# First attention, last four units: the mask under the scores written by TensorE in place of ScalarE

## The chip, the cores and the metric

The kernel runs on one core of one Trainium2 chip. The metric is the device time of the program in microseconds (us), the median of several executions. Five engines run their own instruction streams and meet at semaphores: TensorE (PE) multiplies matrices and writes to PSUM, VectorE (DVE) and ScalarE (ACT) do elementwise work and reductions, GpSimd (POOL) some elementwise work, SyncE (SP) issues DMAs.

## What is computed

One decoder layer on 16 sequences of 128 tokens, model width 256, in three parts, each added to x: a self-attention, a cross-attention to a context, and a mixture of 16 experts with a shared expert. The change touches only the self-attention, called first attention here:

```python
q = (x @ Wq) -> 16 heads of 128;  k, v = (x @ Wk), (x @ Wv) -> 4 heads of 128;  rope on q and k
q1, q2 = halves of q;  k1, k2 = halves of k
s1 = q1 k1^T / 8;  s2 = q2 k2^T / 8
allowed = (j <= i) & (j >= i - 63)
s1, s2 = where(allowed, s, -1e30)
a1, a2 = softmax(s1), softmax(s2)
diff = relu(a1 - lam[head] * a2)
diff = diff / (sum(diff) + 1e-6)
x = x + (diff v) @ Wo
```

The mask lets a token see itself and the 63 before it. It enters as a sum: PSUM holds 0 or -1e30 for each score, and the score products are added to it.

## The kernel before, in words

First attention goes over 4 groups of heads (4 query heads share a key and value head), and in each group over 16 units, one for each sequence. The groups are written as a first one, a loop over the middle ones, and a final one. Four units make a chunk; while one chunk is attended, TensorE projects the keys, queries and values of the next in the gaps between a unit's steps ("slots" 0, 1 and 2 of a unit). The last chunk of the final group has no next one. Its slots hold the start of the next stage: the layer norm's transposes ("ln"), the merging of the cross-attention's weights ("prep", six steps, TensorE lines L690 and L698, taken by ScalarE into wbh and by VectorE into wbl or mq), and transposes of the context ("kt2", L567).

A unit has two score maps, s1 and s2, of 384 columns each: early queries see only 64 keys, so the map of 4 heads is 128 partitions by 384. Each of the two maps has its own bank, and two pairs of banks (A_S) take turns, so unit u writes to those of unit u-2. In the order in which a unit n goes through the engines:

- TensorE, slot 0, then the 16 score products (L647; the profile counts 32, since each is done in two passes), added to the mask that lies in PSUM; then the transposes of the weights of unit n-2 (L661, L663), slot 1, the product with the values for unit n-2 (L670), the output projection of unit n-3 (L679), slot 2.
- VectorE: the difference of the two maps of unit n-1 (L1072), then the negated maxima of unit n (L1126, L1127), then what the slots need.
- ScalarE: the copy pt of the transposed weights (L1401), the clipping with its sum of unit n-1 (L1478), the 8 exponentials of unit n with their sums (L1434), the copy oah of the output (L1401), and last the copy of the mask into the banks just read (L1489, shown as L1401, since all copies go through one helper).
- GpSimd: the normalisation of unit n-2 (L1665), for which TensorE's transposes wait.

The order is written out by hand in each engine's stream; each engine takes its instructions strictly in that order. The mask copy of unit n serves unit n+2: it raises the semaphore a_mk, for which TensorE waits before the scores (the line `wait(pe, a_mk, n - 1)`). The mask copy itself waits for the exponentials of its own unit (a_ex). Only the first two units of all have no earlier unit to write their mask. For these TensorE writes it by a product of the identity with the mask in bf16 (L643), which starts the sum; the score products then add to it. The last two units of the final group write no mask, since none follows.

Of the kernel before, what the change touches and what calls it, by code (L numbers as in the profile page):

```python
# [18 lines left out]
CB = 4  # L19
NC = B // CB  # L20
# [3 lines left out]
UN = B  # L24
# [75 lines left out]
def wait(eng, sem, value):  # L100

    if isinstance(value, int) and value <= 0:
        return
    eng.wait_ge(sem, value)


def decoder_kernel(nc, x, ctx_in, in_wqk, in_wv, in_wo, in_lam, in_taba, in_rawb, in_tabb, in_kvtab,
# [5 lines left out]
    def sem(name):  # L113
        return ctx.enter_context(nc.semaphore(name))
# [4 lines left out]
    with ctx:  # L119
# [106 lines left out]
        def bank(n):  # L226
            return ps[:, n, :]

        def quads(ap):
            return ap.rearrange("p (h k) -> p h k", k=S)  # L230
# [17 lines left out]
        a_sc, a_mx, a_ex = sem("a_scores"), sem("a_negmax"), sem("a_exp")  # L248
        a_mk = sem("a_mask_in_place")
# [50 lines left out]
        def a_part(first, final, drain):  # L300
            return "first" if first else "final" if final else "drain" if drain else ""
# [90 lines left out]
        def early(ap):  # L392
            return ap[..., 0:XP * QH].rearrange("... (p k) -> ... p k", k=QH)

        def late(ap):
            return ap[..., XP * QH:SW].rearrange("... (p k) -> ... p k", k=S)
# [128 lines left out]
        def _(pe):  # L525
# [8 lines left out]
            def ln_turn(m, kt, bk):  # L534

                pe.wait_ge(ln_xt, m + 1)
                for j in range(CB):
                    last = pe.transpose(quads(bank(bk))[:, j, :], xnt[:, m % 2, j, 128 * kt:128 * (kt + 1)], idf[:, :])
                last.then_inc(ln_tp, 1)

            def ln_ready(m):
                pe.wait_ge(ln_l, m + 1)
                pe.wait_ge(ln_l2, m + 1)
# [11 lines left out]
            def pj_taken(what):  # L555
                if what[0] == "ln":
                    pe.wait_ge(ln_h, 2 * what[1] + what[2] + 1)
                elif what[0] == "prep":
                    pe.wait_ge(b_if, what[1] + 1)
                else:  # L560
                    pe.wait_ge(b_kvc, what[1] + 1)

            def b_turn(r):

                pe.wait_ge(b_kv, 5)
                for j in range(CB):
                    last = pe.transpose(quads(bank(PJ))[:, j, :], kvr[:, CB * r + j, :, :], idf[:, :])  # L567
                last.then_inc(b_kvp, 1)
# [26 lines left out]
            def a_unit(g, u, first=False, final=False, drain=False):  # L595
                n, c, j = g * UN + u, u // CB, u % CB

                def slot(s):
                    if not drain and (j, s) in A_SLOT and not (final and c == NC - 1):
                        ahead = c == NC - 1  # L600
                        if held:
                            pj_taken(held.pop())
                        if first and not ahead and A_SLOT[j, s] == 0:
                            ln_ready(c + 1)
                        a_project(g + 1 if ahead else g, (c + 1) % NC, A_SLOT[j, s], ahead)
                    for what in A_EXTRA.get((a_part(first, final, drain), u, s), []):
                        if what[0] == "qb":
                            if what[1] == 0:
                                pe.wait_ge(a_ex, NG * UN)
                                ln_ready(NC)  # L610
                            b_do(0, 0, what, XT + what[1])
                            continue
                        if held:
                            pj_taken(held.pop())
                        else:

                            ahead = [i for k, i in A_SLOT.items() if k <= (j, s)]
                            if final and c == NC - 1:
                                ahead = []
                            pe.wait_ge(a_pf, (g * NC + (c + 1)) * AW + len([i for i in ahead if i != AV]))  # L620
                            pe.wait_ge(a_vf, g * NC + (c + 1) + (AV in ahead))
                        if what[0] == "ln":
                            ln_turn(what[1], what[2], PJ)
                        elif what[0] == "prep":
                            b_prep(0, what[1], bank(PJ)).then_inc(b_it, 1)
                        else:
                            b_turn(what[1])
                        held.append(what)
                slot(0)
                if first and u == 1:  # L630
                    for kt in range(KT):
                        ln_turn(2, kt, OB + kt)
                if not drain:
                    if j == 0:
                        pe.wait_ge(a_pf, (g * NC + (c + 1)) * AW)
                        pe.wait_ge(a_vf, g * NC + (c + 1))
                        pe.wait_ge(a_kd, 64 * (g * NC + (c + 1)))
                    wait(pe, a_mk, n - 1)
                    tok = slice(S * j, S * (j + 1))
                    for m in range(2):  # L640
                        sc = A_S[u % 2][:, m, 0:SW]
                        if first and u < 2:
                            pe.matmul(sc, idb[:, :], maskb[:, :], start=True, stop=False, skip_group_check=True)  # L643
                        for at, to, keys in ((QH, late(sc), S), (0, early(sc), QH)):
                            for h in range(HG):
                                rows = slice(QH * (h % 2), QH * (h % 2) + QH)
                                last = pe.matmul(to[rows, h // 2, :],  # L647
                                                 qab[:, c % 2, m, h, S * j + at:S * j + at + QH],
                                                 kva[:, c % 2, m, S * j:S * j + keys],
                                                 start=False, stop=at == 0, skip_group_check=True)  # L650
                    last.then_inc(a_sc, 1)
                two = not (first and u < 2) and not (drain and u >= 2)
                if two:
                    pe.wait_ge(a_dn, n - 1)
                    wait(pe, a_pt, n - 2)
                    if first and u == 2:
                        pe.wait_ge(ln_h, 2 * 2 + KT)
                    if first and u == 2:
                        pe.wait_ge(a_ptz, 1)
                    for p in range(XP):  # L660
                        pe.transpose(quads(bank(PTB))[0:QH, p, :], early(ea[:, u % 2, 0, :])[:, p, :], idf[:, :])  # L661
                    for p in range(XP):
                        last = pe.transpose(quads(bank(PTB))[:, XP + p, :], late(ea[:, u % 2, 0, :])[:, p, :], idf[:, :])  # L663
                    last.then_inc(a_tp, 1)
                slot(1)
                if two:
                    w = (u - 2) % UN
                    pe.wait_ge(a_pt, n - 1)
                    wait(pe, a_ol, n - 2)
                    pe.matmul(bank(OB), quads(kva[:, (w // CB) % 2, 2, :])[:, w % CB, :],  # L670
                              pt[:, u % 2, :, :], start=True, stop=True).then_inc(a_pv, 1)
                if not (first and u < 3):
                    if u == 3:
                        pe.wait_ge(a_wol, g + 1)
                    pe.wait_ge(a_ol, n - 2)
                    wait(pe, a_y, n - 3)
                    for h in range(HG):
                        for i, (o_, w_) in enumerate(((oah, woh), (oah, wol), (oal, woh))):
                            last = pe.matmul(ps[:, YB, 0:DM], o_[:, (u - 3) % 2, h, :], w_[:, h, :],  # L679
                                             start=h == 0 and i == 0, stop=h == HG - 1 and i == 2)  # L680
                    last.then_inc(a_wo, 1)
                slot(2)
# [716 lines left out]
        def _(act):  # L1399
            def copy(dst, src):  # L1400
                return act.activation(dst, src, ACT.Copy)  # L1401
# [36 lines left out]
            def a_unit(g, u, first=False, final=False, drain=False):  # L1438
                n, c, j = g * UN + u, u // CB, u % CB
# [43 lines left out]
                if two:  # L1483
                    act.wait_ge(a_pv, n - 1)
                    wait(act, a_wo, n - 3)
                    copy(by_head(oah[:, (u - 2) % 2, :, :]), by_block(bank(OB))).then_inc(a_o, 1)
                if not drain and not (final and u >= UN - 2):
                    act.wait_ge(a_ex, n + 1)
                    copy(A_S[u % 2][:, :, 0:SW], maskb[:, :].unsqueeze(1).broadcast_to([128, 2, SW])).then_inc(a_mk, 1)  # L1489
                if first and u == 1:  # L1490
# [439 lines left out]
```

## Time and profile before

| | us |
|---|---|
| median of 3 runs | 1346.26 |
| lowest, highest | 1346.21, 1348.62 |
| span of the profiled execution (first to last instruction) | 1343.3 |
| TensorE, ScalarE, VectorE, GpSimd busy | 1269.2, 715.6, 843.1, 470.9 |
| mask copies of ScalarE, 62 | 52.8 |

Of the profiled execution the profile gives the span and no time of its own that counts what lies outside of it; the median of the runs is 3.0 us above the span. Times in the rows are us from the start of the span. First attention ends at about 502 us, and its final group's last four units are between 443 and 486 us. PE's busy time counts overlapping products by a modelled end, so the distance from one start to the next says more of its pace than the durations. The granted clock of TensorE is 1.00 at 2.4 GHz and 0.50 at 1.2 GHz.

### The profile page before, as it was taken

The page shows a single profiled execution, that of the slowest core. Times are in us where ns is not written, and L with a number is a line of the kernel's source. Part 1 is how long each engine was busy: PE and PEld are TensorE (multiplying, and loading weights), DVE is VectorE, ACT ScalarE, POOL GpSimd, SP SyncE. Part 2 cuts the span into 40 slices and gives each one's busy share as a digit, 9 for nine tenths or more (in the row PEclk, how much of TensorE's full clock was granted, in tenths as well). Part 3 has the DMA queues.
Part 4 walks back from the last instruction along what each step waited for, and adds up shares of the span by engine and source line. Part 5 has one row for each costly group of instructions (what it writes and reads, how often), then busy time and mean ns, then how long its engine had stood idle before and what let it go on. Part 6 is the DMA issues. An engine that isn't in the chain of part 4 may idle for free.

```text
span 1343.3 us, 27486 instructions
## 1 busy us (share of the span) xinstructions
PE 1269.2 (94%) x9712; PEld 989.2 (74%) x9712; DVE 843.1 (63%) x1986; ACT 715.6 (53%) x2746; POOL 470.9 (35%) x467
## 2 busy tenths in 40 slices
PE   5799999999999788999999999989899999999998
PEld 4578888888887565666666666557788888888887
DVE  6788888888888676666656656765453333433333
ACT  2788888889887553444444444465232332423322
POOL 3122113112212134544544534541053353533532
PEclk9999999999999899999999999999999999999999
DMA  6011001100102101002002001000325342254230
GB/s 221 16 25 49 18 17 25 49 17 17 31 19 92 35 1 76 1 1 76 1 1 75 1 1 60 1 1 1 107 58 142 74 120 56 39 137 78 56 93 31
DMA packets 29810, 64.54 MB, mean 48 GB/s; under 512 B 6912, under 2 KB 12160, under 8 KB 28416
## 3 DMA queue, kind: packets, MB, share of 16 engines
q1 hardware_dynamic: 29696, 63.05, 17.6%
q8 instruction: 67, 1.10, 0.3%
q14 instruction: 47, 0.39, 0.1%
HBM read 52.42 MB, written 2.23 MB: 41 GB/s over the span
## 4 chain that ended last, share of the span: by engine, by line
PE 74%; DVE 10%; ACT 7%; issue 4%; POOL 2%; DMA 2%; SPq 1%; DVEq 0%; POOLq 0%; ACTq 0%
PE ps L531 31%; PE ps L923 9%; PE ps L647 5%; PE ps L716 4%; PE ps L679 4%; PE ps L820 4%; ACT ea L1434 3%; PE ps L810 3%; PE ps L792 3%; PE ps L800 2%; PE ps L670 2%; PE ps L586 2%; DMA cw<-comb_d 2%; ACT ea L1478 1%; DVE xnt L991 1%
## 5 line engine op out<-in xcount | busy, mean ns | idle before, releaser
L1798 POOL TENSOR_TENSOR sg<-sg,cw 128x512 f32<-128x512 f32 x88 | 113.5, 1290 | 260.1 <-ACT sg L1597 253.1
L1375 DVE TENSOR_TENSOR hh<-ps,sg 128x512 f32<-128x512 f32 x100 | 69.2, 692 | 178.6 <-POOL sg L1798 162.0
L1401 ACT ACTIVATE hhh<-hh 128x512 fp32r<-128x512 f32 x100 | 63.2, 632 | 214.7 <-DVE hh L1375 214.7
L1401 ACT ACTIVATE pt<-ps 128x512 f32<-128x512 f32 x128 | 76.9, 600 | 179.3 <-PE ps L800 122.6
L1434 ACT ACTIVATE ea<-ps,negmax 128x64 f32<-128x64 f32 (+1 forms) x512 | 164.6, 341 | 6.0 <-DVE negmax L1127 6.0
L531 PE MATMUL ps<-xnh,wch 128*128 128x512 f32 x400 | 157.0, 393 | 0.7 <-ACT pt L1401 0.7
L1174 DVE TENSOR_TENSOR qcs<-ps,tabb 128x512 f32<-128x512 f32 x192 | 123.6, 686 | 53.4 <-PE ps L531 53.1
L531 PE MATMUL ps<-xnl,wch 128*128 128x512 f32 x400 | 156.9, 392 | 0.0
L531 PE MATMUL ps<-xnh,wcl 128*128 128x512 f32 x400 | 155.6, 389 | 0.0
L1665 POOL TENSOR_TENSOR ea<-ea,rden 128x128 f32<-128x128 f32 (+1 forms) x128 | 62.1, 506 | 256.2 <-DVE rden L1083 256.2
L1672 POOL TENSOR_TENSOR eb<-eb,rsum 128x512 f32<-128x512 f32 x64 | 66.9, 1045 | 160.3 <-DVE rsum L1218 160.3
L923 PE MATMUL ps<-wch,hhh 128*128 128x256 f32 x400 | 115.9, 290 | 4.7 <-DVE hhl L1377 2.4
L1377 DVE TENSOR_TENSOR hhl<-hh,hhh 128x512 fp32r<-128x512 f32 x100 | 75.5, 755 | 69.8 <-ACT hhh L1401 69.8
L923 PE MATMUL ps<-wch,hhl 128*128 128x256 f32 x400 | 113.6, 284 | 0.0
L923 PE MATMUL ps<-wcl,hhh 128*128 128x256 f32 x400 | 113.6, 284 | 0.0
L1434 ACT ACTIVATION_READ_ACCUMULATOR ea<-ps,negmax 128x1 f32 x512 | 107.1, 209 | 0.0
L1434 ACT ACTIVATE eb<-ps,negmax 128x128 f32<-128x128 f32 x256 | 90.5, 368 | 29.4 <-DVE negmax L1212 29.1
L1088 DVE TENSOR_TENSOR x_sb<-ps,x_sb 128x256 f32<-128x256 f32 x128 | 54.1, 423 | 82.1 <-PE ps L820 58.4
L647 PEld LDWEIGHTS ps<-kva,qab 128*64 128x64 f32 x2048 | 93.2, 139 | 13.1 <-issue 7.9
L647 PE MATMUL ps<-kva,qab 128*64 128x128 f32 (+1 forms) x2048 | 102.4, 254 | 0.0
L679 PE MATMUL ps<-woh,oah 128*128 128x256 f32 x256 | 97.6, 381 | 0.7 <-DVE oal L1118 0.7
L1597 ACT ACTIVATE sg<-ps 128x512 f32<-128x512 f32 x100 | 59.9, 599 | 71.5 <-PE ps L531 70.6
(153 smaller groups left out, 3349.6 us busy)
## 6 DMA issues: line engine op xcount, KB each, us to landing
raw_w<-in_rawb_dram SPq DMA_DIRECT2D x4, 2432.0 KB, 9.0
kva<-ktmp SPq DMA_DIRECT2D x64, 128.0 KB, 2.4
cw<-comb_d SPq DMA_DIRECT2D x32, 256.0 KB, 5.0
raw_w<-in_rawc_dram SPq DMA_DIRECT2D x4, 1920.0 KB, 8.0
cw<-comb_d SPq DMA_DIRECT2D x16, 224.0 KB, 4.3
raw_a<-in_wqk_dram SPq DMA_DIRECT2D x4, 768.0 KB, 5.4
cw<-comb_d SPq DMA_DIRECT2D x16, 192.0 KB, 6.0
cw<-comb_d SPq DMA_DIRECT2D x16, 160.0 KB, 5.5
```

The lines of the kernel that those rows point to most:

```text
L531: last = pe.matmul(out_ap, w, m, start=n == 0, stop=n == len(steps) - 1)
L647: last = pe.matmul(to[rows, h // 2, :], qab[:, c % 2, m, h, S * j + at:S * j + at + QH], kva[:, c % 2, m, S * j:S * j + keys], start=False ...
L679: last = pe.matmul(ps[:, YB, 0:DM], o_[:, (u - 3) % 2, h, :], w_[:, h, :], start=h == 0 and i == 0, stop=h == HG - 1 and i == 2)
L923: last = pe.matmul(ps[:, j // 2, DM * (j % 2):DM * (j % 2 + 1)], h_[:, par, S * j:S * (j + 1)], w_[:, t, 2 * KT * 128:RC_T], start=begin a ...
L1174: last = dve.tensor_tensor(quads(qcs[:, t, m, :]), quads(bk), bcast(tabb[:, b_table(t), m, :]), ALU.mult)
L1375: dve.tensor_tensor(hh[:, par, :], bank(C_U[par]), sg[:, par, :], ALU.mult).then_inc(c_h, 1)
L1377: dve.tensor_tensor(hhl[:, par, :], hh[:, par, :], hhh[:, par, :].bitcast(f32), ALU.subtract)\
L1401: return act.activation(dst, src, ACT.Copy)
L1434: last = act.activation(dst(m, h), src, ACT.Exp, bias=negmax[:, par, i:i + 1], accum_out=sums[:, par, i:i + 1])
L1665: last = pool.tensor_tensor(part, part, rden[:, par, XP * i:XP * (i + 1)].unsqueeze(2) .broadcast_to([128, XP, (QH, S)[i]]), ALU.mult)
L1672: pool.tensor_tensor(src[:, par, :, :], src[:, par, :, :], rec[:, par, :].unsqueeze(2).broadcast_to([128, HG, S]), ALU.mult).then_inc(done, 1)
L1798: pool.tensor_tensor(sg[:, par, :], sg[:, par, :], cw[:, c % 2, t, :], ALU.mult).then_inc(c_hs, 1)
```

## The change

In the final group, TensorE writes the mask of units 12 to 15 by the product that the first two units use, two products a unit, one for each map. ScalarE's copies behind units 10 to 13 of that group, which wrote it, are left out. For these units TensorE waits for the exponentials of the unit two before (a_ex), since a_mk is not raised for them. `CB` is 4, `UN` 16 and `NC` 4.

```diff
--- before.py
+++ after.py
@@ -635,11 +635,15 @@
                         pe.wait_ge(a_pf, (g * NC + (c + 1)) * AW)
                         pe.wait_ge(a_vf, g * NC + (c + 1))
                         pe.wait_ge(a_kd, 64 * (g * NC + (c + 1)))
-                    wait(pe, a_mk, n - 1)
+                    by_pe = (first and u < 2) or (final and c == NC - 1)
+                    if final and c == NC - 1:
+                        wait(pe, a_ex, n - 1)
+                    else:
+                        wait(pe, a_mk, n - 1)
                     tok = slice(S * j, S * (j + 1))
                     for m in range(2):
                         sc = A_S[u % 2][:, m, 0:SW]
-                        if first and u < 2:
+                        if by_pe:
                             pe.matmul(sc, idb[:, :], maskb[:, :], start=True, stop=False, skip_group_check=True)
                         for at, to, keys in ((QH, late(sc), S), (0, early(sc), QH)):
                             for h in range(HG):
@@ -1484,7 +1488,7 @@
                     act.wait_ge(a_pv, n - 1)
                     wait(act, a_wo, n - 3)
                     copy(by_head(oah[:, (u - 2) % 2, :, :]), by_block(bank(OB))).then_inc(a_o, 1)
-                if not drain and not (final and u >= UN - 2):
+                if not drain and not (final and u >= UN - CB - 2):
                     act.wait_ge(a_ex, n + 1)
                     copy(A_S[u % 2][:, :, 0:SW], maskb[:, :].unsqueeze(1).broadcast_to([128, 2, SW])).then_inc(a_mk, 1)
                 if first and u == 1:
```

ScalarE's stream in the final group, behind the exponentials of unit 10 and then of unit 11. The names read out<-in; kva takes the values of the last chunk, wbh the high part of the merged weights. Before:

```order
L1401 ACTIVATE oah<-ps 128x2x4x64
L1401 ACTIVATE ps<-maskb 128x2x384
L1401 ACTIVATE kva<-ps 128x512
L1401 ACTIVATE xnf<-ps 128x512
L1401 ACTIVATE xnh<-ps 128x512
...
L1401 ACTIVATE oah<-ps 128x2x4x64
L1401 ACTIVATE ps<-maskb 128x2x384
L1401 ACTIVATE wbh<-ps 128x4x64
L1401 ACTIVATE wbh<-ps 128x4x32
L1401 ACTIVATE pt<-ps 128x512
```

After:

```order
L1405 ACTIVATE oah<-ps 128x2x4x64
L1405 ACTIVATE kva<-ps 128x512
L1405 ACTIVATE xnf<-ps 128x512
L1405 ACTIVATE xnh<-ps 128x512
...
L1405 ACTIVATE oah<-ps 128x2x4x64
L1405 ACTIVATE wbh<-ps 128x4x64
L1405 ACTIVATE wbh<-ps 128x4x32
L1405 ACTIVATE pt<-ps 128x512
```

The two mask copies are gone, and kva and wbh follow oah directly; two more go likewise behind units 12 and 13.

TensorE's stream around the scores of unit 12, from the merging product of prep 0 to that of prep 1. Before:

```order
L690 MATMUL ps<-raw_w 128x192 x2
L647 MATMUL ps<-kva,qab 64x128 x4
L647 MATMUL ps<-kva,qab 64x64 x4
L647 MATMUL ps<-kva,qab 64x128 x4
L647 MATMUL ps<-kva,qab 64x64 x4
L661 MATMUL ps<-idf,ea 64x128 x2
L663 MATMUL ps<-idf,ea 128x128 x2
L690 MATMUL ps<-raw_w 128x192 x2
```

After:

```order
L694 MATMUL ps<-raw_w 128x192 x2
L647 MATMUL ps<-maskb,idb 128x384
L651 MATMUL ps<-kva,qab 64x128 x4
L651 MATMUL ps<-kva,qab 64x64 x4
L647 MATMUL ps<-maskb,idb 128x384
L651 MATMUL ps<-kva,qab 64x128 x4
L651 MATMUL ps<-kva,qab 64x64 x4
L665 MATMUL ps<-idf,ea 64x128 x2
L667 MATMUL ps<-idf,ea 128x128 x2
L694 MATMUL ps<-raw_w 128x192 x2
```

A mask product stands ahead of each map's score products; the same holds for units 13, 14 and 15. From L647 on, TensorE's line numbers are higher by four in the changed kernel. The instructions of the other engines keep their order.

## Rows read from the trace of the kernel before

**Rows 1.** The page: the chain that ended last, by engine.

```profile
PE 74%; DVE 10%; ACT 7%; issue 4%; POOL 2%; DMA 2%; SPq 1%; DVEq 0%; POOLq 0%; ACTq 0%
```

**Rows 2.** The mask's instructions: count, ns min/median/max, first and last start us.

```profile
L1401 ACT ACTIVATE ps<-maskb x62: 814/850/882, 35.8 to 462.5; 128x768 f32<-128x768 bf16 x62
```

**Rows 3.** The chain of waits, units 10 to 15: start us, us, what.

```profile
428.09 1.38 PE ps L531 x6
...
433.55 0.80 issue
...
442.75 0.70 ACT ps L1401
...
465.88 1.71 PE ps L698 x20
467.58 2.76 PE ps L647 x32
470.34 0.57 PE ps L661 x2
470.91 0.44 PE ps L663 x2
...
477.28 1.49 PE ps L647 x32
```

**Rows 4.** ScalarE's timeline: start us, us, instruction, idle before and its releaser.

```profile
432.89 0.85 ACT L1401 ACTIVATE ps<-maskb 128x768 f32<-128x768 bf16 x1
433.62 0.63 ACT L1401 ACTIVATE kva<-ps 128x512 f32<-128x512 f32 x1
...
442.57 0.88 ACT L1401 ACTIVATE ps<-maskb 128x768 f32<-128x768 bf16 x1
443.43 0.55 ACT L1401 ACTIVATE wbh<-ps 128x256 fp32r<-128x256 f32 x2
445.48 0.60 ACT L1401 ACTIVATE pt<-ps 128x512 f32<-128x512 f32 x1 [1.49 <-PE ps L663]
446.32 0.26 ACT L1478 ACTIVATE ea<-ea 128x64 f32<-128x64 f32 x1 [0.25 <-DVE ea L1072]
...
452.95 0.55 ACT L1401 ACTIVATE wbh<-ps 128x256 fp32r<-128x256 f32 x2 [1.25 <-PE ps L690]
...
471.38 0.60 ACT L1401 ACTIVATE pt<-ps 128x512 f32<-128x512 f32 x1 [7.98 <-PE ps L663]
471.87 0.25 ACT L1478 ACTIVATE ea<-ea 128x64 f32<-128x64 f32 x1
```

**Rows 5.** TensorE's timeline, the first unit of all, and what follows it.

```profile
29.50 0.32 PE L643 MATMUL ps<-maskb,idb 128*128 128x384 bf16 x1 [1.69 <-DVE qab L1032]
...
30.58 0.34 PE L643 MATMUL ps<-maskb,idb 128*128 128x384 bf16 x1
...
31.66 0.50 PE L531 MATMUL ps<-xnh,wah 128*128 128x512 f32 x1
```

**Rows 6.** TensorE's timeline, units 10 to 13 of the final group.

```profile
431.60 1.95 PE L586 MATMUL ps<-wv,xnf 128*128 128x128 f32 x16
...
442.58 0.81 PE L690 MATMUL ps<-raw_w 128*128 128x192 f32 x4
...
451.28 1.63 PE L690 MATMUL ps<-raw_w 128*128 128x192 f32 x4 [2.61 <-DVE wbl L1181]
452.84 2.46 PE L647 MATMUL ps<-kva,qab 128*64 128x128 f32 x32
456.36 0.41 PE L661 MATMUL ps<-idf,ea 128*64 128x128 f32 x2 [1.07 <-POOL ea L1665]
```

**Rows 7.** Busy time by stretch: us, PE busy, granted clock, DMA share, GB/s.

```profile
453.00:454.00 1.00, 1.00 (x14) 0.50 0.04 8
466.00:468.00 2.00, 2.00 (x25) 0.50 0.00 0
472.00:473.00 1.00, 1.00 (x4) 1.00 0.00 0
```

## The prediction

> **What bounds the kernel now.** I read the chain of waits of the whole program first. TensorE holds 74% of it and ScalarE 7% [rows 1], so work added to TensorE costs time unless a wait covers it, and work taken from ScalarE gives something only where ScalarE is late. Then I listed the instructions that read the mask: 62 mask copies of 850 ns each, the last at 462.5 [rows 2]. The change removes the last four of them, so 3.4 us of ScalarE's time is the most that could come back. Which of the four is on the path is read from the chain over the last units of first attention [rows 3]: it names a mask copy once, for 0.70 us at 442.75, and an "issue" of 0.80 us at 433.55, behind which a second one could hide. So I looked at each copy's neighbours in ScalarE's timeline [rows 4].
>
> **What is removed.** I call the last sixteen units 0 to 15; the removed copies stand behind the exponentials of units 10 to 13, and fed units 12 to 15. The wait of TensorE that each satisfied never ended last: a copy starts two units ahead of its scores (432.89 against scores behind the product of 442.58, 462.5 against 477.28) [rows 2, 3, 4, 6]. What counts is the ScalarE instruction behind each copy.
> - Copy at 432.89: the next one, the copy of the values into kva, starts 0.73 us later, at 433.62 [rows 4], which looks as if it waited for the mask copy. But the projection that it reads starts at 431.60 and takes 1.95 us, so it ends at 433.55 [rows 6]. Without the mask copy it would start 0.07 us earlier at most, and less the 0.04 us that such a release takes (452.91 to 452.95 below), 0.03 us. TensorE's transposes behind the "issue" wait for that copy. Gain 0.03.
> - Copy at 442.57: the next, wbh, starts at 443.43 [rows 4]. The product that it reads starts at 442.58 and takes 0.81 us, so it ends at 443.39 [rows 6]; 0.04 us later wbh starts. The same distance stands where wbh was plainly waiting for TensorE: idle 1.25 us, ended by L690 at 452.95 [rows 4], whose product ran from 451.28 for 1.63 us, to 452.91 [rows 6]. So here TensorE released it, and the 0.70 us that the chain charges to the mask copy is not to be had. Gain 0; bound above, 0.12 us: a mask copy alone holds its follower for 0.73 to 0.74 us, which would be 443.31.
> - Copies behind units 12 and 13: ScalarE is idle behind them, 1.25 us until 452.95 and 7.98 us until 471.38 [rows 4]. Gain 0.
>
> The sum of the gains is 0.03 us, between 0 and 0.15.
>
> **What is added.** Eight products, mask by identity, 128x384 in bf16, two ahead of each of units 12 to 15, with their weight loads. The first units have the same pattern. There a map with its mask product takes from 29.50 to 30.58 = 1.08 us, and the unit of two maps from 29.50 to 31.66 = 2.16 us [rows 5]. A unit without them takes 1.49 us at 477.28 [rows 3]. So a pair costs 2.16 - 1.49 = 0.67 us of TensorE at full clock. At the lower one, the 32 score products take 2.76 us in place of 1.49 [rows 3], a factor of 1.85, so the pair costs 0.67 x 1.85 = 1.24 us; the bound is twice, 1.34.
>
> Against this stands a rule of the Trainium skill. "TensorE: Matmul & The Clock Gate", section "Back-to-back issue gap", gives N / 2.4 + 2.5 ns between starts at full clock and N / 1.2 at the low one. For 384 columns that is an estimate of 0.16 and 0.32 us a product, and half of what the rows show for the pair. The trace's first units measure this very sequence and include what the change of operands does to the score products behind it, so I go by them; the cheaper result is a rival below.
>
> Unit by unit, in TensorE's order, with what covers it:
> - Unit 12 (scores behind the product of 442.58, full clock): +0.67 on the transposes and on ScalarE's copy pt at 445.48. Behind it ScalarE's clipping starts at 446.32, having waited for VectorE's difference. With VectorE out of the way it starts 0.49 us after pt (471.38 to 471.87). So the cover is 0.84 - 0.49 = 0.35 us [rows 4], and 0.67 - 0.35 = 0.32 us passes to the exponentials and through them to wbh and VectorE's chain up to unit 13. VectorE's maximum is behind that same difference, so it hides the later scores.
> - Unit 13 (scores at 452.84, low clock at first): TensorE is idle 1.07 us behind the scores until GpSimd's normalisation ends [rows 6]. The pair costs at most 1.24. The clock is at 0.50 in 453 to 454 [rows 7], and rises in the midst of the scores, whose 32 took 2.46 us and not 2.76 [rows 3, 6], so part of the pair's cost falls at full clock. I take 0, with 0.17 (1.24 - 1.07) as the upper bound.
> - Unit 14 (scores at 467.58, low clock): the chain runs through the product of prep, the scores, both pairs of transposes and ScalarE [rows 3], with nothing idle. The pair costs 1.24. The clock is at 0.50 in 466 to 468 and 1.00 in 472 to 473 [rows 7]; work pushed past the rise runs faster. The transposes would be pushed there: 0.57 + 0.44 = 1.01 us [rows 3], and 1.01 / 1.85 = 0.55 at full clock, which is 0.46 to get back at most. I take half, so 1.24 - 0.23 = 1.01, between 0.67 and 1.34.
> - Unit 15 (scores at 477.28, full clock): on the chain with the transposes and ScalarE behind them [rows 3]. +0.67.
>
> Nothing behind waits for a fixed time, and TensorE leads the chain from there on, so a shift at the end of the stage is carried to the end. No DMA is moved. The new wait, for the exponentials of two units before, was implied by the old one, and queues nothing new.
>
> **Sum.** -0.03 + 0.32 + 0 + 1.01 + 0.67 = +1.97 us. The profiled execution spans 1343.3 us, and the median of the runs is 1346.26, 3.0 us more, which I take to stay. The forecast is 1346.26 + 1.97, about 1348.2 us, 0.15% slower. With the bounds, the sum is 0.67 at the least for unit 14 and 1.34 at the most: -0.15 + 0.32 + 0 + 0.67 + 0.67 = 1.5, up to 0.32 + 0.17 + 1.34 + 0.67 = 2.5, so 1347.8 to 1348.8, and somewhat wider, 1347.3 to 1349.3, for the spread of the runs. What a measurement of this kernel can tell from no change is 0.2%, 2.7 us; the forecast is within it.
>
> **Rivals.**
> - The product is cheap. Six projections of 512 columns take 1.38 us, 0.23 each from 428.09 [rows 3]; 384 columns at that rate are 0.17 us, 0.35 the pair, and 0.35 x 1.85 = 0.64 at the low clock. Then unit 12's is just covered, unit 13's too, and 0.64 + 0.35 = 1.0: 1347.2 us. For it: nothing but the first units shows the dear one. Against it: both maps of the first unit take the same 1.08 us [rows 5], so it was no accident of the first product. The gap formula of the Trainium skill, "TensorE: Matmul & The Clock Gate", would lead to this case.
> - The added work prolongs the low clock (the slower side). Place: unit 14. If the clock has not risen by the time that unit 15 starts, then unit 15's scores take 2.76 in place of 1.49, its pair 1.24 and its transposes 0.46 more. In sum 0.32 + 1.24 + 1.27 + 1.24 + 0.46 = 4.5: 1350.8 us, 0.34% slower. It decides from the point where the granted clock is below 1.00 at the scores of unit 15. Against it: TensorE is busier there than before, and the clock was back at 1.00 in 472 to 473, four us ahead of unit 15's scores [rows 3, 7].
> - The clock stays up ahead of unit 14, since TensorE is busier. The chain's stretch from 465.88 is at the low clock, behind one in which TensorE did little. At full clock the scores save 1.27, the transposes 0.46, prep's products 1.71 - 1.71 / 1.85 = 0.79 [rows 3], and the pair costs 0.67: 0.32 + 0.67 + 0.67 - 2.52 = -0.9: 1345.4 us. Against it: the change adds nothing to TensorE's work between unit 13's scores and 465.88.
> - The copies were on the path as the chain says: 0.73 and 0.70 us come back, and the products are mostly covered by the idle time so won (left 0.3): 1346.26 - 1.43 + 0.3 = 1345.1 us. Against it: the 0.04 us distances above.
>
> **Chances.** Forecast 0.60, cheap product 0.14, longer low clock 0.12, clock stays up 0.08, copies on the path 0.06. Faster by over 0.2% (below 1343.6) none of the cases reaches; 0.04 for what I don't see. Slower by over 0.2% (above 1348.95): the 0.12, and a fifth of the forecast's, 0.12, so 0.24. Within: 0.72. The range 1345.3 to 1349.8 leaves out most of the longer low clock and little at the lower end; the likeliest case's own is 1347.3 to 1349.3.
>
> **What would show it.** In the profile after: eight more products of mask by identity beside the four, 58 mask copies of some 850 ns. Unit 12 to its transposes 2.16 us in place of 1.49, and the clipping behind it waiting for VectorE no longer. wbh still 0.04 us behind the product that it reads: if it starts a good 0.1 us earlier, the copy was late after all. TensorE's wait for GpSimd at unit 13 shrunk from 1.07 but not gone. Units 14 and 15 longer by 1.2 and 0.67. The start of unit 15's last exponentials against unit 10's some 2 us later than before. The forecast is wrong if the granted clock of 465 to 480 has other low stretches than before, or if the pair costs near 0.35.

## The result and the profile after

| | median, us | lowest to highest | runs | ratio to before, 95% |
|---|---|---|---|---|
| before | 1347.05 | 1346.08 to 1348.62 | 7 | |
| changed | 1351.11 | 1348.68 to 1352.11 | 7 | 1.0026, 1.0017 to 1.0036 |

The ratios here and below are not the quotients of the two medians, and differ from them by up to 0.06%, 0.8 us; here the quotient is 1.0030.

The change makes the kernel slower by 0.26%, where 0.15% was forecast, and the median lies 1.3 us above the upper end of the range. The spans rose from 1343.3 to 1350.3 us, but the profiled execution of the changed kernel was its slowest, 1352.11 us. The first lines of the page, and the chain by engine, answer to [rows 1]:

```profile
span 1350.3 us, 27498 instructions
...
PE 72%; DVE 10%; ACT 8%; issue 4%; DMA 3%; POOL 2%; SPq 1%; DVEq 0%; POOLq 0%; ACTq 0%
```

What the changed kernel's trace says of the mask answers to [rows 2] (ns min/median/max, first and last start):

```profile
L1405 ACT ACTIVATE ps<-maskb x58: 814/852/863, 36.4 to 428.4; 128x768 f32<-128x768 bf16 x58
...
L647 PE MATMUL ps<-maskb,idb x12: 323/337/527, 29.5 to 482.4; 128*128 128x384 bf16 x12
```

Four copies are gone and eight products have come. The longest of the products, 527 ns, is not one at full clock: the four of the kernel before took 322 to 337 ns. The chain of waits shows where they stand (start us, us, what); it answers to [rows 3]. The first row is a stretch ahead of everything that was changed:

```profile
423.85 2.56 PE ps L531 x6
...
446.22 0.16 PE ps L647
446.38 0.82 PE ps L651 x16
447.20 0.27 PE ps L647
447.47 0.82 PE ps L651 x16
...
470.65 0.43 PE ps L647
471.08 1.48 PE ps L651 x16
472.56 0.43 PE ps L647
473.00 1.48 PE ps L651 x16
474.48 0.38 PE ps L665 x2
474.86 0.23 PE ps L667 x2
...
481.03 0.16 PE ps L647
481.19 1.29 PE ps L651 x16
482.48 0.43 PE ps L647
482.92 1.48 PE ps L651 x16
484.40 0.54 PE ps L665 x2
```

A unit's pair shows as two L647 rows, its scores as two L651 rows. Unit 12 takes 446.22 to 448.29 on the chain with everything at full clock. Unit 14, from 470.65 to 474.48, takes 3.83 us against 2.76. Unit 15, from 481.03 to 484.40, takes 3.37 us against 1.49 [rows 3]. In unit 12 the second product takes 0.27 us and each half of the scores 0.82; in unit 15 they take 0.43, 1.29 and 1.48. TensorE's clock fell within its first half. The granted clock by stretch (us, PE busy, clock, DMA share, GB/s) answers to [rows 7]:

```profile
424.00:426.00 2.00, 2.00 (x6) 0.50 1.41 320
470.60:474.50 3.90, 3.90 (x39) 0.50 0.00 0
475.20:478.00 2.80, 2.55 (x16) 1.00 0.03 6
480.40:481.30 0.90, 0.90 (x9) 1.00 0.00 0
482.00:485.00 3.00, 3.00 (x32) 0.54 0.00 0
```

The low stretch at unit 14 is there as before. The one of 482 to 485, over unit 15's scores, is new. In the kernel before, unit 15's scores ran in full clock:

```profile
476.60:479.20 2.60, 2.58 (x41) 1.00 0.00 0
```

ScalarE's timeline answers to [rows 4], with the one row of before that was not shown, unit 15's pt:

```profile
436.49 0.60 ACT L1405 ACTIVATE kva<-ps 128x512 f32<-128x512 f32 x1 [0.75 <-PE ps L586]
...
446.26 0.55 ACT L1405 ACTIVATE wbh<-ps 128x256 fp32r<-128x256 f32 x2 [0.67 <-PE ps L694]
448.88 0.60 ACT L1405 ACTIVATE pt<-ps 128x512 f32<-128x512 f32 x1 [2.07 <-PE ps L667]
449.38 0.25 ACT L1482 ACTIVATE ea<-ea 128x64 f32<-128x64 f32 x1
...
475.11 0.60 ACT L1405 ACTIVATE pt<-ps 128x512 f32<-128x512 f32 x1 [9.36 <-PE ps L667]
...
485.19 0.60 ACT L1405 ACTIVATE pt<-ps 128x512 f32<-128x512 f32 x1 [3.04 <-PE ps L667]
```

```profile
479.37 0.60 ACT L1401 ACTIVATE pt<-ps 128x512 f32<-128x512 f32 x1 [0.96 <-PE ps L663]
```

TensorE's timeline answers to [rows 6], and its last row shows the idle gap ahead of unit 15. Below it stands the same row of before, with the same gap:

```profile
434.50 1.95 PE L586 MATMUL ps<-wv,xnf 128*128 128x128 f32 x16
...
445.41 0.81 PE L694 MATMUL ps<-raw_w 128*128 128x192 f32 x4
...
459.42 0.41 PE L665 MATMUL ps<-idf,ea 128*64 128x128 f32 x2 [0.64 <-POOL ea L1669]
...
480.37 0.66 PE L538 MATMUL ps<-idf,xnt 128*128 128x128 f32 x4 [2.05 <-ACT xnh L1405]
```

```profile
476.62 0.66 PE L538 MATMUL ps<-idf,xnt 128*128 128x128 f32 x4 [2.04 <-ACT xnh L1401]
```

With these rows the difference can be followed from place to place (starts in us):

| place | before | changed | shift |
|---|---|---|---|
| projection of the values, unit 10 | 431.60 | 434.50 | 2.90 |
| prep's first product, unit 11 | 442.58 | 445.41 | 2.83 |
| pt, unit 12 | 445.48 | 448.88 | 3.40 |
| clipping, unit 12 | 446.32 | 449.38 | 3.06 |
| transposes, unit 13 | 456.36 | 459.42 | 3.06 |
| pt, unit 14 | 471.38 | 475.11 | 3.73 |
| pt, unit 15 | 479.37 | 485.19 | 5.82 |
| span | 1343.3 | 1350.3 | 7.0 |

So 2.9 us had gone before the first changed instruction, and 1.2 us go behind the last one, all of it between 1000 and 1200 us, where the later traces lose anything from 0 to 0.9 against before (e3 below, which has no added product, 0.8). In the changed units the trace loses 5.82 - 2.90 = 2.92 us: +0.23 at unit 12 after a gain of 0.07, 0 at unit 13, +0.67 at unit 14, and +2.09 at unit 15.

The executions of a kernel differ in where TensorE's clock is low. The runs give the mean granted clock of each: of the kernel before, 0.989 to 0.993, mean 0.990 over 27 runs; of the changed kernel, in 13 runs of two measurements, 0.988 eleven times, 0.989 once, and 0.992 in its fastest run of 1348.68 us. The profiled execution of before was of a rarer kind: its clock is 0.993, as in 6 of those 27 runs (timed with e1 to e4), whose median is 1345.4 us, against 1347.2 for the 20 runs at 0.989 or 0.990. The comparison of medians takes this in; a single trace does not.

### The profile page after: what moved, and what is told of

It reads as the page before. It is cut to its first block, busy times and chain, and to the rows that moved or that the text cites. A ratio compares the mean times of both kernels' runs of the same rounds, so it can differ in the third digit from the quotient of the medians.

```text
span 1350.3 us, 27498 instructions
## 1 busy us (share of the span) xinstructions
PE 1277.0 (95%) x9720; PEld 993.5 (74%) x9720; DVE 842.9 (62%) x1986; ACT 713.3 (53%) x2742; POOL 471.1 (35%) x467
## 4 chain that ended last, share of the span: by engine, by line
PE 72%; DVE 10%; ACT 8%; issue 4%; DMA 3%; POOL 2%; SPq 1%; DVEq 0%; POOLq 0%; ACTq 0%
PE ps L531 30%; PE ps L927 8%; PE ps L651 5%; PE ps L720 4%; PE ps L824 4%; PE ps L683 4%; ACT ea L1438 3%; PE ps L814 3%; PE ps L796 3%; PE ps L674 3%; PE ps L804 2%; DMA cw<-comb_d 2%; PE ps L586 2%; ACT ea L1482 1%; POOL sg L1802 1%
## 5 line engine op out<-in xcount | busy, mean ns | idle before, releaser
L651 PEld LDWEIGHTS ps<-kva,qab 128*64 128x64 f32 x2048 | 94.8, 141 | 14.6 <-issue 9.4
L651 PE MATMUL ps<-kva,qab 128*64 128x128 f32 (+1 forms) x2048 | 104.8, 256 | 0.0
```

The costliest lines, as they stand in the source:

```text
L651: last = pe.matmul(to[rows, h // 2, :], qab[:, c % 2, m, h, S * j + at:S * j + at + QH], kva[:, c % 2, m, S * j:S * j + keys], start=False ...
```

## The experiments

Two theories stood after the result. A: the products cost their own time on the path, about 1.6 us, and the rest are low stretches of the clock which fall where they fall. B: the change itself brings the low stretch onto unit 15. Each kernel was timed in five rounds beside the kernel before; the ratio is that to it.

| kernel | median, us | before, us | ratio, 95% | mean clock of its runs |
|---|---|---|---|---|
| e1_after_again | 1350.32 | 1346.47 | 1.0030, 1.0018 to 1.0042 | 0.988 |
| e2_copies_kept | 1348.78 | 1346.47 | 1.0020, 1.0011 to 1.0030 | 0.991 |
| e3_neither | 1346.81 | 1346.47 | 1.0003, 0.9994 to 1.0012 | 0.989 |
| e4_early | 1346.10 | 1346.47 | 1.0003, 0.9994 to 1.0012 | 0.990 |
| e5_after_filled | 1347.30 | 1346.83 | 0.9998, 0.9989 to 1.0007 | 0.993 |
| e6_early_filled | 1345.05 | 1346.83 | 0.9983, 0.9974 to 0.9992 | 0.994 |
| e7_unit14_only | 1350.78 | 1346.83 | 1.0024, 1.0016 to 1.0033 | 0.987 |
| e8_unit15_only | 1347.10 | 1346.83 | 1.0001, 0.9992 to 1.0010 | 0.990 |
| e9_unit14_early | 1348.40 | 1347.08 | 1.0008, 0.9999 to 1.0017 | 0.990 |
| e10_fill_one_gap | 1349.47 | 1347.08 | 1.0021, 1.0012 to 1.0030 | 0.989 |
| e11_early_filled_again | 1344.81 | 1347.08 | 0.9988, 0.9979 to 0.9997 | 0.993 |

### The changed kernel again

No edit.

> The changed kernel once more, unaltered. Theory A (direct cost of the mask products on the path, about 1.6 us, plus low stretches of TensorE's clock that fall at places the change does not touch and differ by chance from execution to execution): the time is 1349 to 1351, and the trace shows other low stretches than the first trace of the changed kernel; in particular the 2.9 us that it had lost before the first changed instruction are gone or different. Theory B (the change itself moves the low stretch onto unit 15): 1350.5 to 1352, and a low stretch at unit 15's scores again.

The loss is no accident of the first measurement. In this trace the changed units lose 3.13 us, against 2.92 in the first, and a low stretch lies on unit 15 again:

```profile
480.50:483.70 3.20, 3.20 (x30) 0.50 0.00 0
```

From pt of unit 14 to pt of unit 15 it loses 1.94 us, 2.09 in the first. This speaks for B. The median of 1350.32 us lies in A's range and 0.2 below B's, and the loss ahead of the change is 1.2 us here and not 2.9, as A said of it. So each theory had a part of it right.

### The products alone, the copies alone

```diff
 e2, in the kernel before:
-                        if first and u < 2:
+                        if (first and u < 2) or (final and c == NC - 1):
 e3, in the changed kernel:
-                    by_pe = (first and u < 2) or (final and c == NC - 1)
+                    by_pe = first and u < 2
```

> The kernel before with TensorE's eight mask products added ahead of units 12 to 15, while ScalarE's four mask copies stay. If the products carry the whole cost, the time is that of the changed kernel (ratio to before 1.0015 to 1.003). If leaving out the copies costs or gains anything, this run differs from the changed kernel by it: my prediction says 0.03 us, the rival that the copies were on the path says 1.4 us slower than the changed kernel.

> The changed kernel without the eight mask products: the scores of units 12 to 15 of the final group are added to what stands in PSUM, with no fresh mask. It shows what the removal of the copies is worth by itself. Theory A and B: the time of before, ratio 1.000 within 0.001, no low stretch at unit 15's scores. Copies on the path: 1.4 us faster, ratio 0.999. If something else than the products made the changed kernel slow (the new wait, the placing of the code), this one is slow as well: ratio 1.002 or more.

e3 leaves out the mask under the scores of units 12 to 15, and so does not compute attention as defined; its scores are added to what stands in PSUM. Its time is that of before: leaving out the four copies is worth nothing that the runs can tell, and neither is the new wait. With the products and the copies the kernel is slow again, at 1.0020, whose interval overlaps with those of the changed kernel. So the products carry the cost, or most of it: the median of e2 is 1.5 us below that of e1, and five of its ten runs have a mean clock of 0.992, where all six of e1 have 0.988. Why was not tested. The profiled execution of e2, its fastest, had no low stretch at unit 14, and none at unit 15, though the pair of unit 14 and the idle gap ahead of unit 15 (2.06 us) are there:

```profile
458.00:461.00 3.00, 3.00 (x8) 0.50 0.00 0
462.00:495.00 33.00, 23.46 (x206) 1.00 0.00 0
```

```profile
467.12 0.34 PE L643 MATMUL ps<-maskb,idb 128*128 128x384 bf16 x1
```

Unit 14's scores with their pair took 2.17 us there (467.12 to the transposes at 469.29), so the price of a pair at full clock is the same at this place as in the first units.

The trace of e3 also answers where more than half of the 2.9 us ahead of the change comes from. It has the instructions of before up to there and beyond, and a low clock at the same place as the changed kernel, the projections of unit 9:

```profile
421.20:424.40 3.20, 3.20 (x9) 0.50 1.02 232
```

It loses 1.6 us there, and seven of the other experiments' traces lose 1.5 to 1.7. The profiled execution of the kernel before was one without that stretch. Of the other 1.3 us, 1.1 had gone by 60 us, where the changed kernel's trace has three low stretches (from 30.8, 37.6 and 51.3 us) and that of before one (from 48.6). Neither is a part of what the change does.

### The products in idle time

```diff
 e4, in the changed kernel:
+            def mask_early(g, u):
+                pe.wait_ge(a_ex, g * UN + u - 1)
+                for m in range(2):
+                    pe.matmul(A_S[u % 2][:, m, 0:SW], idb[:, :], maskb[:, :], start=True, stop=False,
+                              skip_group_check=True)
...
+                    if final and (u, s) == (11, 1):
+                        mask_early(g, 12)
...
-                    by_pe = (first and u < 2) or (final and c == NC - 1)
+                    by_pe = first and u < 2
...
+                if final and u in (12, 13, 14):
+                    mask_early(g, u + 1)
                 slot(2)
```

> The changed kernel with each pair of mask products issued earlier, where TensorE is idle: for unit 12 in unit 11 ahead of its second layer-norm transposes, for units 13 to 15 behind the output projection of units 12, 13 and 14. The products cost the same but lie in idle time. Both theories: the direct cost goes, ratio to before 1.000 within 0.001; 1.6 us less than the changed kernel by the direct cost alone, 3 to 4 us less if the low stretch at unit 15 goes with it. If the products' place does not matter, it stays at 1.0026.

As expected: the median is 4.2 us below that of the changed kernel in the same measurement. The same eight products cost nothing where TensorE idles. In the trace no unit from 11 to 15 loses or gains over 0.15 us against before, and unit 15 runs at full clock.

### One unit alone

```diff
 e7:
+                    by_pe = (first and u < 2) or (final and u == 14)
+                    if final and u == 14:
...
+                        wait(pe, a_mk, n - 1 - (final and u == 15))
...
+                if not drain and not (final and u in (12, 14, 15)):
 e8:
+                    by_pe = (first and u < 2) or (final and u == 15)
+                    if final and u == 15:
...
+                if not drain and not (final and u >= 13):
```

> Of the change only unit 14: TensorE writes its mask, ScalarE's copy behind unit 12 is left out, the other three copies stay. Direct cost 0.67 to 1.1 us. If shifting unit 14 is what brings the low stretch to unit 15's scores, that stretch shows here as well, though unit 15 has no product: unit 15's scores take 2 to 2.7 us in place of 1.49, and the total is 1348.3 to 1349. If the product of unit 15 itself is needed, the total is 1347.2 to 1347.6 and unit 15's scores take 1.49.

> Of the change only unit 15: TensorE writes its mask, ScalarE's copy behind unit 13 is left out. Direct cost 0.67 us at full clock: 1347.2, ratio 1.0005. If the low stretch comes only through the shift of unit 14, none is at unit 15's scores here; if it comes through unit 15's own product, the pair and the scores take up to 3.8 us and the total is 1348.5 to 1349.

This decides for B, and says which pair it is. With unit 14's pair alone the kernel is as slow as with all four, 1.0024. TensorE's timeline and its clock in e7, where unit 15 has no product:

```profile
479.89 0.66 PE L538 MATMUL ps<-idf,xnt 128*128 128x128 f32 x4 [2.06 <-ACT xnh L1405]
480.48 2.32 PE L651 MATMUL ps<-kva,qab 128*64 128x128 f32 x32
482.73 0.64 PE L665 MATMUL ps<-idf,ea 128*64 128x128 f32 x2
```

```profile
480.50:481.00 0.50, 0.50 (x11) 1.00 0.00 0
481.20:484.40 3.20, 3.20 (x30) 0.50 0.00 0
```

Unit 15's scores take 480.48 to 482.73 = 2.25 us in place of 1.49, and the clock is at 0.50 from within them on. Its pt starts 1.21 us later than unit 14's shift accounts for. The median, 1350.78, lies 1.8 us above the upper end of what was expected. The trace has one more low stretch, from 498.1 us on, over projections of the next stage, which costs 1.5 us; that it lies there in the other runs too was not seen, but nine of the twelve have a mean clock of 0.986 or 0.987, below any of the changed kernel. With unit 15's own pair alone, e8, nothing of it:

```profile
479.24 0.66 PE L538 MATMUL ps<-idf,xnt 128*128 128x128 f32 x4 [2.04 <-ACT xnh L1405]
479.74 0.33 PE L647 MATMUL ps<-maskb,idb 128*128 128x384 bf16 x1
...
481.90 0.41 PE L665 MATMUL ps<-idf,ea 128*64 128x128 f32 x2
```

```profile
479.20:482.40 3.20, 3.16 (x43) 1.00 0.00 0
```

The idle gap ahead of the transposes at 479.24 is 2.04 us, as long as in e7 (2.06) and in the changed kernel (2.05), so its length does not tell the two apart. What differs is the added pair in unit 14, 1.07 us at the low clock there. The pair of unit 15 costs 479.74 to 481.90 = 2.16 us against 1.49, the 0.67 of the prediction; 0.09 of it comes back in the distance between the transposes and the scores (0.50 us against 0.59), so 0.58 passes on.

### Unit 14's pair moved, and one gap filled

```diff
 e9, with mask_early as in e4:
+                    by_pe = (first and u < 2) or (final and c == NC - 1 and u != 14)
...
+                if final and u == 13:
+                    mask_early(g, u + 1)
 e10, in the changed kernel, with a third argument that repeats the pair:
+                if final and u == 14:
+                    mask_early(g, u + 1, 5)
```

> The changed kernel with one pair moved: unit 14's mask products are issued in unit 13, behind its output projection where TensorE is idle; the pairs of units 12, 13 and 15 stay in front of their scores. Theory A (unit 14's pair in front of its scores delays what follows, and that brings the low stretch to unit 15): no low stretch at unit 15's scores, unit 15's scores with their pair take 2.16 us, and of the change 0.2 + 0.6 = 0.8 us is left: 1347.3 to 1348, about 3 us below the changed kernel. Theory B (any three of the four pairs bring the low stretch, by their total): it stays at 1349.5 to 1351.

> The changed kernel with all pairs in place and only the idle gap before unit 15 (unit 14, behind its output projection) filled by five repeats of the pair. Theory A (unit 15's low stretch follows the idle of 2.05 us ahead of it): the low stretch at unit 15 goes, its scores with the pair take 2.16 us, and the time is 1348 to 1349, 1.5 to 2.3 us below the changed kernel. If the low stretch has nothing to do with that gap, it stays at 1350 to 1351.

In both traces the low stretch at unit 15 is gone. For unit 14's pair this agrees with e7 and e8: the three traces with a low unit 15 (the changed kernel twice, e7) have the pair in front of unit 14's scores, and no trace without it has one. From prep's first product in unit 11 to pt of unit 15, e9's trace loses 0.79 us, the 0.8 that Theory A left. That the idle gap is needed too rests on the trace of e10, and is not shown: e2's trace has pair and gap and a full clock at unit 15, and e10's profiled execution (mean clock 0.992, as two of its eleven runs) is not of the kind of the seven at 0.988 or 0.989. But in both traces another one has come in its place, over the projections at the start of the next stage, where the kernel before had none:

```profile
477.10:480.20 3.10, 3.10 (x43) 1.00 0.00 0
496.00:499.00 3.00, 3.00 (x9) 0.50 0.00 0
```

```profile
478.00:481.20 3.20, 3.17 (x43) 1.00 0.00 0
496.30:499.50 3.20, 3.20 (x10) 0.50 0.02 5
```

It costs 1.6 us there in each. In e10 the fill cuts the idle time ahead of unit 15 to 0.41 us:

```profile
475.82 1.80 PE L598 MATMUL ps<-maskb,idb 128*128 128x384 bf16 x10
478.03 0.66 PE L538 MATMUL ps<-idf,xnt 128*128 128x128 f32 x4 [0.41 <-ACT xnh L1413]
```

but the time stays at 1.0021: the expected 1348 to 1349 was missed by 0.5 us. For e9, the median of 1348.4 is 0.4 above what was expected, and its interval reaches to no change. So taking away one low stretch does not give back its price; it may fall elsewhere. In how many executions it does was not measured, since only one of each kernel has a profile.

### All gaps filled

```diff
 e5, in the changed kernel, with the third argument of e10:
+                if final and u == 14:
+                    mask_early(g, 14, 5)
                 slot(0)
...
+                if final and u in (12, 13, 14):
+                    mask_early(g, u + 1, {12: 5, 13: 7, 14: 5}[u])
 e6 and e11: the same in e4
```

> The changed kernel, with TensorE's idle gaps in units 12 to 14 of the final group filled by repeats of the same mask products into the bank that the next unit uses (5, 7, 5 and 5 pairs), while the products in front of the scores stay. Theory A (products cost their own time, and on top of it low stretches of the clock behind the idle gaps make units 14 and 15 longer): the clock stays at 1.00 from unit 12 to 15, the products cost 0.23 + 0.67 + 0.67 = 1.6 us on the path and the held clock gives back the 2.5 us of unit 14 and the low stretch at unit 15: 1345.5 to 1346.5, 4 to 5 us below the changed kernel. Theory B (the products cost more than their time on the path and the clock has no part in it): no change to the changed kernel, 1350 to 1351. Should the fillers be too long for the gaps, it is slower than that.

> As the filled kernel, but without the products in front of the scores: the mask is written by the early pairs in the idle gaps alone, and those of unit 12 in unit 11. Theory A: 1.6 us less than the filled kernel with the products in front, so 1344 to 1345 and faster than the kernel before by 2 to 3 us (ratio 0.998). Theory B: as the early kernel, 1346 to 1346.5, ratio 1.000.

> The filled kernel with all pairs early, once more, to see whether it beats the kernel before: ratio 0.998 again (0.9975 to 0.999), and in the trace no low stretch from unit 12 to unit 15. If the first measurement was luck of the executions, the ratio is 1.000.

With the pairs in front of the scores and 44 more products in the gaps, e5, the changed kernel's loss is gone: 0.9998. Its runs were expected at 1345.5 to 1346.5 and came at 1347.30, where its trace still has a low stretch at unit 13's output projection and the one at unit 9. With the pairs early as well, the kernel beats both: 0.9983, and 0.9988 in the second measurement, some 2 us below before. The same fill in the kernel before, with ScalarE's copies left as they are, was not run. The clock of e11:

```profile
451.00:490.00 39.00, 32.10 (x281) 1.00 0.02 4
490.00:500.00 10.00, 7.86 (x50) 1.00 0.01 2
```

The trace of e6 has none up to 490 either, but one from 494.8 on. In e11 there is none from unit 12 into the next stage, and pt of unit 14 comes 2.4 us earlier against unit 13's than in the kernel before, close to what the prediction had priced (2.52) for a clock that stays up there.

## Why the prediction was wrong

- **The copies.** Right. In the changed trace kva starts 0.04 us behind the end of the product that it reads (434.50 + 1.95 = 436.45, 436.49), and wbh too (445.41 + 0.81 = 446.22, 446.26). The 0.70 us that the chain of before charged to the mask copy did not come back. kva starts 0.03 us nearer to the product's end than before, which is the gain that was said. The transposes behind it start another 0.03 nearer, which makes the 0.07 above, but e7 and e8, which keep the copy behind unit 10, show the same, so it is no clear gain of the change.
- **The price of a pair.** Right at full clock: 446.06 to 448.22 = 2.16 us in unit 12 (the mask product starts 0.16 us ahead of its row on the chain), 2.16 in e8. Of these 0.67 us, 0.09 come back, since the pair starts that much nearer to the work ahead of it, so 0.58 passes on; the prediction did not have this. At the low clock it was 3.83 - 2.76 = 1.07 us, where 1.24 was estimated. The gap rule of the Trainium skill ("TensorE: Matmul & The Clock Gate", "Back-to-back issue gap") gives 0.16 and 0.32 us a product. The trace does not agree for this sequence: 0.25 to 0.27 us at full clock and 0.43 at the low one from the product's start to that of the scores, and slower scores behind, so the rival of the cheap product falls. For the same product repeated it does agree: the ten fillers of e10 start 0.16 us apart (475.82 to 477.29 for nine steps).
- **Unit 12.** Right: 3.06 - 2.83 = 0.23, where 0.32 was said. The cover behind pt was 0.35 as predicted; the difference is the 0.09 above.
- **Unit 13.** Right: the wait for GpSimd shrank from 1.07 to 0.64 us and passed nothing on.
- **Unit 14.** +0.67, where 1.01 was taken, at the lower bound: the transposes took 0.61 us in place of 1.01, so nearly all of the 0.46 came back, not half. That is one execution: e1's trace has +1.04 there and e7's +0.84, so the 1.01 was a fair value.
- **Unit 15. The step that failed:** "Unit 15 (scores at 477.28, full clock): on the chain [...] +0.67." The size at full clock was right. That the clock is full there was taken from the trace of before and not bounded. It cost 2.09 us, 0.58 by the pair and 1.5 by the low stretch (1.94 us in e1's trace, so 1.4 by the stretch). e7 shows that the pair of unit 14 brings that stretch, with no product in unit 15 at all; e8 that unit 15's own does not.
- **The rival of the longer low clock** was the nearest in number, by luck, at 1350.8 us against a measured 1351.11, and its sign to look for was met, the granted clock below 1.00 at unit 15's scores. Its mechanism was not: the low stretch of unit 14 ended by 475.2, the clock was at 1.00 up to 481.3, and then a new one came. Of its terms 1.24 us for unit 14 and 2.97 for unit 15 stand against 0.67 and 2.09. My argument against it, that TensorE is busier there than before, was no argument, since TensorE idles 2.05 us ahead of unit 15 in both kernels, and what I added lay before that gap. It had a chance of 0.12, too little.
- **The sum** of the terms as measured is -0.07 + 0.23 + 0 + 0.67 + 2.09 = 2.92 us, within the 2.3 to 4.8 us that the ratio's interval makes of 1347. The medians lie 4.06 apart. What makes up the remaining 1.1 us is open. A further low stretch in some executions would do it: e1's trace of the changed kernel has one, from 948 to 955 us, twice as long as the one that before has near there, and loses 0.7 us by it. Whether the change brings it is not shown; e9's trace has it too, the other traces do not.
- **The spread.** I took the one profiled execution of before as the pattern of its low stretches, and the 3.0 us between its span and the median as what lies outside of the span. Every run on record is 1.8 or 1.9 us above its own span, so the other 1.2 us are that this execution, with some 1345.1 us, was faster than all seven runs of before. Nine of the twelve later traces, e3's among them, show one at unit 9 that it did not have.

What decides whether the clock falls in unit 15 or stays is open too. The experiments show that unit 14's pair brings the fall, though not in every execution (e2's trace), and that the clock stayed up in the traces with the idle time ahead of unit 15 filled; not by what measure.

## What to carry to other kernels

Where TensorE alternates short idle gaps with work and the trace has a low stretch of its clock nearby, an added pair of products can cost 1.2 to 1.5 us more in the next unit: bound every later term of the sum at both clocks, not only the unit in which the low one stands. Put such small products where TensorE idles anyway. There they cost nothing that the runs can tell (e4), and repeated to fill the gaps they bought 2 us (e6, e11). A line that the chain of waits names is late only if its follower was not about to be held by something else; compare its start with the end of what it reads.

## What the runs showed of the hardware

- Identical work at one place ran at the full or at the low clock in different executions: unit 14's scores with their pair 2.17 us in e2, 3.83 us in the changed kernel.
- An idle gap of 2.04 to 2.06 us ahead of unit 15 was followed by a low clock in the changed kernel and e7, and by full clock in the kernel before, e2 and e8. No idle gap of TensorE between 440 us and unit 15 was longer than 2.8 us in any trace, and low stretches lie there all the same.
- A low stretch that was removed at one place came up at another (unit 15 to the projections of the next stage, e9 and e10).
- A bf16 product of 384 columns between fp32 products of other weights takes 0.25 to 0.27 us to the next start at full clock and 0.43 at the low one. Ten of them in a row start 0.16 us apart at full clock (e10). The 16 score products behind one take 0.82 us against 0.745 (half of 1.49).
